# When Pool takes a power, and when it scatters: the graph stage of a decoder

## The chip, the cores and the metric

One core of a Trainium2 chip runs the whole network in one launch. The metric is the device time in microseconds of that launch, as the median of three runs. The engines have queues of their own and run in order: TensorE (PE), VectorE (DVE), ScalarE (ACT), GpSimd (Pool) and SyncE (SP), which issues most of the transfers. They meet only at semaphores.

## The reference, cut to what matters

The network is two decoder layers on x of shape (4, 512, 512). The change touches one stage, the graph attention of the first layer and the routing of the mixture of experts that follows it, for each of 4 batches of 512 rows:

```python
sim = einsum('bhnd,bhmd->bnm', Q, K) / (sqrt(d) * H)
threshold = top_k(sim, int(512 * 0.3))[0][:, :, -1:]      # the 153rd largest of each row
A = sigmoid(sim) * (sim >= threshold)
A = (A + swapaxes(A, -1, -2)) * 0.5
x = x + (1 - gamma) * layernorm(x) + gamma * A            # layernorm(x) stands for adj_raw
scores = softmax(layernorm(x) @ w_cls.T)                  # 64 experts, 32 of them real
_, choice = top_k(scores + bias, 8)                       # 8 experts a row
```

The normalised rows go to the slots of their experts, 8 copies of each.

## The kernel before

The stage is the function graph_and_router. A batch is four tiles of 128 rows. PE makes the similarities, and the 153rd largest of each row is found in two ways at once. For tiles 0 and 1 (COUNTED) it is found by halving: ACT counts in 32 rounds (TESTS) how many similarities lie above a test value (`count`, L1896, two instructions a round, one for each tile), and after each count Pool moves the test (`update`, L2220 to L2236, two to four small instructions a tile). For tiles 2 and 3 DVE takes the eight largest and strikes them out, 20 times (`strike_out`, L2000 and L2006). The search of batch b + 1 is interleaved with the rest of batch b's work on DVE by an order written out by hand in `finish` and `router`.

DVE's order for a batch b is: `blend_statistics(b)`, the mean and variance of x (the last instruction is L2025); `blend_x(b)`, which waits for Pool's power and makes the sum of x and its normalised self (L2034 to L2044); `exact_bounds(b)`, which waits for the last update of batch b (the flags, L2051); `adjacency(b)` (L2069, L2072); two rounds of the next search; `add_adjacency(b)`, which waits for PE's transposed adjacency; the statistics of the new x; two more rounds; `normalize(b)`, which waits for Pool's second power (L2089); five rounds; the router, from the logits (L2125) to the slots (L2184); the remaining rounds. In the last batch there is no next search.

Pool raises the variances to the power -1/2 in `rstds(b, k)` (L2240), k = 0 for x and k = 1 for the x with the adjacency added. It also sends the normalised rows to their slots: `scatter` (L2248) is an indirect DMA of 128 rows, and there are 32 for each batch. The 32 of batch b are spread over the rounds of the next two batches: ten go behind rounds 22 to 31 (LATE) of batch b + 1, the rest in the early rounds (EARLY) of batch b + 2. For the last two batches what is left goes behind the last round. ACT also copies, in its order, the queries, keys and similarities of batch b + 1 behind round 4 of batch b (round 2 of batch 0), the transposed x, the logits and the exponentials of batch b - 1 behind rounds 9, 11 and 13, and results of other weight work that fills PE (`keep_aside`, behind rounds 18 to 29). PE runs in the order of the batches: transposed adjacency, similarities of batch b + 2, logits, counts of choices, weight work. SP reloads x for the next batch behind `blend_x` and stores the sum behind `add_adjacency`.

The stage ends when all scatters have landed. The experts' stage reads the slots.

Of the kernel before, what the change touches and what calls it, by code (L numbers as in the profile page):

```python
# [16 lines left out]
B, S, D = 4, 512, 512  # L17
T = B * S
NT = S // P
# [1523 lines left out]
def graph_and_router(nc, env, tag, x_in, x_out, ctx_in, wq, wk, gamma, w_cls, bias, slot_rows, none_row, slots, weights, w1, w3, w2, hadamard, w13T, w2T, late_jobs, first_gu, first_d, shared_x, shared_rows, w_gate_up, w_down):  # L1543

    with semaphores(nc) as take, ExitStack() as ctx:
# [424 lines left out]
        def _(dve):  # L1970
# [94 lines left out]
            def adjacency(b):  # L2065
                for t in range(NT):
                    dve.wait_ge(tanh_done, NT * b + t + 1)
                    least = bound[:, t:t + 1] if t < COUNTED[b] else top[:, t, LAST:LAST + 1]
                    dve.tensor_scalar(sim[:, b % 2, t, :], sim[:, b % 2, t, :], least, gam[:, 2:3], ALU.is_ge, ALU.mult).then_inc(masked, 1)  # L2069
                for t in range(NT):  # L2070
                    dve.wait_ge(masked, NT * b + t + 1)
                    dve.scalar_tensor_tensor(out=adjacent[:, t, :], in0=adjacent[:, t, :], scalar=1.0, in1=sim[:, b % 2, t, :],  # L2072
                                             op0=ALU.add, op1=ALU.mult).then_inc(adj, 1)
# [18 lines left out]
            def finish(b):  # L2092
                exact_bounds(b)
                adjacency(b)
                strike_out(b + 1, 0, 2)
                if b < B - 1:
                    add_adjacency(b)
                    dve.wait_ge(added, NT * (b + 1))
                    carry()
                    statistics(b, 1, xo)  # L2100
                else:
                    for t in range(NT):
                        add_tile(b, t)
                        dve.wait_ge(added, NT * b + t + 1)
                        carry()
                        tile_statistics(1, xo, t)
                    gather_statistics(b, 1)
                strike_out(b + 1, 2, 4)
                normalize(b)
                strike_out(b + 1, 4, 9)  # L2110
                router(b, lambda: strike_out(b + 1, 9, 10), lambda: strike_out(b + 1, 10, ROUNDS + 1))
# [80 lines left out]
            strike_out(0, 0, ROUNDS + 1)  # L2192
            for b in range(B):
                blend_statistics(b)
                blend_x(b)
                finish(b)
            for u, (j, c) in enumerate(late_units):
                high, low = late_jobs[j][1:]
# [8 lines left out]
        def _(pool):  # L2207
# [30 lines left out]
            def rstds(b, k):  # L2238
                pool.wait_ge(stat[k], (2 * NT + 1) * (b + 1))
                pool.tensor_tensor(rstd[:, k, :, 0], mv[:, k, :, 1], env.minus_half[:, 0:NT], ALU.pow).then_inc(rstd_done[k], 1)  # L2240
# [22 lines left out]
            LATE = 22  # L2263
            EARLY = {0: 2, 4: 5, 5: 1, 7: 1, 9: 3, 10: 1, 11: 2, 13: 2, 15: 1, 17: 1, 18: 1, 20: 1, 21: 1}
            assert sum(EARLY.values()) + TESTS - LATE == NT * TOPK
            for b in range(B):
                sent = TESTS - LATE
                for r in range(TESTS):
                    for j in range(COUNTED[b]):
                        update(b, r, j)  # L2270
                    if b and r == 4:
                        rstds(b - 1, 1)
                    if r == (26 if b else 24):
                        rstds(b, 0)
                    if b >= 2 and r in EARLY:
                        scatter(b - 2, sent, sent + EARLY[r])
                        sent += EARLY[r]
                    if b and r >= LATE:
                        if b == 1 and r == LATE:
                            pool.wait_ge(zeroed, 16 * (ZERO_DMAS + 1))  # L2280
                        scatter(b - 1, r - LATE, r - LATE + 1)
            scatter(B - 2, TESTS - LATE, TESTS - LATE + 12)
            rstds(B - 1, 1)
            scatter(B - 2, TESTS - LATE + 12, NT * TOPK)
            scatter(B - 1, 0, NT * TOPK)
            for i in range(2):
                pool.wait_ge(scattered[i], 16 * NT * TOPK * B // 2)
# [611 lines left out]
```

## Time and profile before

| | us |
|---|---|
| median of 3 runs | 3081.89 |
| lowest and highest | 3077.84, 3084.49 |
| the profiled execution | 3076.68 |
| its span, first to last instruction | 3074.7 |
| graph stage, first search to last scatter (of the span) | about 690 to 1196 |
| busy over the span: PE, DVE, ACT, Pool | 2470.5, 1837.2, 1242.4, 859.5 |
| mean granted TensorE clock | 0.893 |

The profile gives for each instruction its engine, start and length in us from the start of the span, and what ended the idle time of its engine before it. Times without another mark are such starts. Idle time of an engine counts only if something waits for the engine later.

### The profile page before, as it was taken

To read this page: it belongs to the slowest core of one execution; us is meant where nothing else is said; L and a number is where in the kernel's file an instruction comes from. 1 tells how busy PE (TensorE), PEld (TensorE's weight loads), DVE (VectorE), ACT (ScalarE), POOL (GpSimd) and SP (SyncE) were. 2 spreads that over 40 slices of the span, in tenths; PEclk is the share of its full clock that TensorE was granted. 3 is DMA by queue.
4 is the path that set the end of the run, shared out by engine and by line. 5 is a ranking of instruction groups with operands and counts; after the bars stand their busy time and mean duration, and the time that the engine had idled before them with its cause. 6 is when DMAs were issued, how large, how long until landed. Compare 5 with 4: busy or idle time off the path is not lost. (4 is left out here: it accounts for less than half of the span.)

```text
span 3074.7 us, 34907 instructions
## 1 busy us (share of the span) xinstructions
PE 2470.5 (80%) x12662; PEld 1631.8 (53%) x12662; DVE 1837.2 (60%) x2917; ACT 1242.4 (40%) x1873; POOL 859.5 (28%) x1198
## 2 busy tenths in 40 slices
PE   5898989863531334999727999999999969999999
PEld 4454545321211223999624545545555537888887
DVE  3756566528977853777556777565555534444443
ACT  2443435328745533666402334334333323333332
POOL 2222223215667755333263333001111110000000
PEclk8999999975665666999858999999999979999999
DMA  4213131226222153899676565333433324001000
GB/s 121 58 43 83 42 82 46 69 103 265 76 70 83 58 166 113 287 304 304 209 188 160 133 178 146 101 83 95 121 100 79 100 74 159 31 11 42 1 28 14
DMA packets 200952, 340.40 MB, mean 111 GB/s; under 512 B 28809, under 2 KB 60425, under 8 KB 198754
## 3 DMA queue, kind: packets, MB, share of 16 engines
q1 hardware_dynamic: 177250, 299.80, 32.3%
q0 software_dynamic: 20480, 37.87, 4.9%
q8 instruction: 86, 1.41, 0.2%
q10 hardware_dynamic: 3072, 0.79, 0.1%
q14 instruction: 64, 0.52, 0.1%
HBM read 182.30 MB, written 109.05 MB: 95 GB/s over the span
## 5 line engine op out<-in xcount | busy, mean ns | idle before, releaser
L670 ACT ACTIVATE at_probs<-at_ps 128x1024 f32<-128x1024 f32 (+3 forms) x256 | 221.8, 866 | 273.7 <-PE at_ps L538 271.0
L757 DVE TENSOR_REDUCE at_negmax<-at_ps 128x2 f32<-128x1024 f32 (+3 forms) x256 | 259.0, 1015 | 122.0 <-PE at_ps L523 64.3
L1367 DVE TENSOR_REDUCE a_negmax<-a_ps 128x2 f32<-128x1024 f32 x128 | 155.1, 1216 | 137.4 <-PE a_ps L1120 136.8
L1896 ACT ACTIVATE gr_act_signs<-gr_signed,gr_test 128x512 bf16<-128x512 f32 x248 | 177.2, 716 | 133.4 <-POOL gr_test L2236 103.1
L59 PE MATMUL ff_ps<-ff_xnT_hi,ff_s_hi 128*128 128x512 f32 x512 | 201.0, 393 | 5.1 <-DVE ff_xnT_lo L2767 5.1
L61 PE MATMUL ff_ps<-ff_xnT_hi,ff_s_lo 128*128 128x512 f32 x512 | 200.2, 391 | 0.0
L60 PE MATMUL ff_ps<-ff_xnT_lo,ff_s_hi 128*128 128x512 f32 x512 | 200.1, 391 | 0.0
L538 PE MATMUL at_ps<-at_qk 98*128 98x512 f32 (+3 forms) x512 | 172.7, 420 | 20.5 <-DMA at_qk<-at_mrow 11.5
L2797 DVE TENSOR_TENSOR ff_hid<-ff_hid,ff_ps 128x512 f32<-128x512 f32 x64 | 44.0, 687 | 238.8 <-ACT ff_hid L2742 238.8
L1268 ACT ACTIVATE a_probs<-a_ps 128x1024 f32<-128x1024 f32 x128 | 131.0, 1024 | 137.1 <-PE a_ps L1138 136.6
L518 PE MATMUL at_ps<-at_qk 96*128 96x512 f32 (+3 forms) x512 | 163.9, 384 | 17.7 <-DVE at_xnT_lo L818 8.0
L538 PEld LDWEIGHTS at_ps<-at_qk 98*128 98x128 f32 x512 | 83.6, 195 | 164.6 <-issue 94.4
L2742 ACT ACTIVATE ff_hid<-ff_ps 128x512 f32<-128x512 f32 x64 | 38.3, 598 | 303.5 <-PE ff_ps L61 303.5
L2539 POOL TENSOR_TENSOR ex_d_lo<-first_d,ex_d_hi 128x1024 fp32r<-128x1024 f32 x32 | 95.9, 2996 | 216.8 <-ACT ex_d_hi L2465 216.8
L59 PE MATMUL ex_ps<-ex_x_hi,ex_gu_hi 128*128 128x256 f32 x512 | 148.3, 290 | 0.0
L61 PE MATMUL ex_ps<-ex_x_hi,ex_gu_lo 128*128 128x256 f32 x512 | 145.6, 284 | 0.0
L60 PE MATMUL ex_ps<-ex_x_lo,ex_gu_hi 128*128 128x256 f32 x512 | 145.6, 284 | 0.0
L2248 POOL DMA_INDIRECT slot_rows<-shared_x,slots x128 | 133.0, 1039 | 39.5 <-issue 39.5
L852 POOL TENSOR_SCALAR_AFFINE_SELECT at_probs<-at_probs 128x256 f32<-128x256 f32 x128 | 52.5, 411 | 292.5 <-ACT at_probs L670 292.5
L782 DVE RECIPROCAL at_weighed<-at_weighed 128x128 f32<-128x128 f32 x128 | 119.7, 939 | 15.5 <-ACT at_weighed L705 15.5
L873 POOL TENSOR_TENSOR at_oT<-at_weighed 128x512 f32<-128x512 f32 x32 | 40.7, 1273 | 296.5 <-DVE at_weighed L782 296.5
L726 ACT CAST at_part<-at_ps 128x512 fp32r<-128x512 f32 x64 | 37.5, 587 | 208.9 <-PE at_ps L61 198.4
(410 smaller groups left out, 6552.9 us busy)
## 6 DMA issues: line engine op xcount, KB each, us to landing
at_qk<-at_part SPq DMA_DIRECT2D x384, 128.0 KB, 2.5
first_gu<-in_L_ffn_w_gate_up_dram SPq DMA_DIRECT2D x32, 1024.0 KB, 5.5
a_qk<-a_part SPq DMA_DIRECT2D x192, 128.0 KB, 2.4
slot_rows<-gr_zeros SPq DMA_DIRECT2D x16, 1024.0 KB
first_d<-in_L_ffn_w_down_dram SPq DMA_DIRECT2D x32, 512.0 KB, 6.4
ex_rows<-slot_rows SPq DMA_DIRECT2D x32, 512.0 KB, 4.5
out_rows<-ex_y SPq DMA_DIRECT2D x32, 512.0 KB, 3.0
gr_aside_raw<-in_L_ffn_W_dram SPq DMA_DIRECT2D x48, 256.0 KB, 3.0
```

The costliest lines, as they stand in the source:

```text
L59: pe.matmul(out, lh, rh, start=start, stop=False, skip_group_check=True)
L60: pe.matmul(out, lh, rl, start=False, stop=False, skip_group_check=True)
L61: return pe.matmul(out, ll, rh, start=False, stop=stop, skip_group_check=True)
L518: mm = pe.matmul(bank(key, i, 0, n), qk[0:KROWS, g % STACKS, 0, j, t * P:(t + 1) * P], qk[0:KROWS, g % STACKS, 1, j, 0:n], start=True, sto ...
L538: mm = pe.matmul(bank(key, i, lo), qk[0:KROWS + 2, g % STACKS, 1, j, t * P:(t + 1) * P], qk[0:KROWS + 2, g % STACKS, 0, j, lo:S], start=Tr ...
L670: act.activation(probs[:, t % 2, 2 * w:2 * w + 2, lo:S], banks(("kq", g, s), lo), ACT.Exp, scale=SCALE).then_inc(free(("kq", g, s)), 1)
L757: dve.reduce_max(negmax[:, g % 2, :].rearrange("p (j t) -> p j t", t=NT)[:, 2 * w:2 * w + 2, t], banks(("qk", g, s), 0, width(g, t)), AX.X ...
L782: dve.reciprocal(weighed[:, 1, t * P:(t + 1) * P], weighed[:, 1, t * P:(t + 1) * P]).then_inc(rec_done, 1)
L1268: act.activation(probs[:, t % 2, 2 * w:2 * w + 2, :], banks(("kq", g, s)), ACT.Exp, scale=SCALE).then_inc(free(("kq", g, s)), 1)
L1367: dve.reduce_max(negmax[:, g % 2, :].rearrange("p (j t) -> p j t", t=NT)[:, 2 * w:2 * w + 2, t], banks(("qk", g, s)), AX.X, negate=True).t ...
L1896: act.activation(act_signs[:, j, :], src, ACT.Sign, scale=-1.0, bias=against, accum_out=total[:, i, j:j + 1]).then_inc(counted_to[j], 1)
L2248: pool.indirect_dma_start(slot_rows, bass.IndirectOffsetOnAxis(slots[:, n:n + 1], 0), xn[:, b % 2, at // TOPK, :], None, bounds_check=SLOT ...
```

## The change

Three things. The order of DVE: `blend_x(b)` comes behind `adjacency(b)` and no longer behind the statistics. Pool's powers: `rstds(b, 0)` leaves round 24 (batch 0) or 26 (others) and follows the last round of its batch; `rstds(b - 1, 1)` goes from round 4 to round 8 in batch 1 and to round 5 in batches 2 and 3. Pool's scatters: in the last batch rounds 22 to 31 send none, and the ten of batch 2 that stood there follow behind the last round and the power. There the order is now `scatter(B - 2, 0, 12)`, the second power, `scatter(B - 2, 12, 32)`, where it was `scatter(B - 2, 10, 22)`, the second power, `scatter(B - 2, 22, 32)`.

```diff
--- before.py
+++ after.py
@@ -2092,6 +2092,7 @@
             def finish(b):
                 exact_bounds(b)
                 adjacency(b)
+                blend_x(b)
                 strike_out(b + 1, 0, 2)
                 if b < B - 1:
                     add_adjacency(b)
@@ -2192,7 +2193,6 @@
             strike_out(0, 0, ROUNDS + 1)
             for b in range(B):
                 blend_statistics(b)
-                blend_x(b)
                 finish(b)
             for u, (j, c) in enumerate(late_units):
                 high, low = late_jobs[j][1:]
@@ -2268,20 +2268,19 @@
                 for r in range(TESTS):
                     for j in range(COUNTED[b]):
                         update(b, r, j)
-                    if b and r == 4:
+                    if b and r == (8 if b == 1 else 5):
                         rstds(b - 1, 1)
-                    if r == (26 if b else 24):
-                        rstds(b, 0)
                     if b >= 2 and r in EARLY:
                         scatter(b - 2, sent, sent + EARLY[r])
                         sent += EARLY[r]
-                    if b and r >= LATE:
+                    if 0 < b < B - 1 and r >= LATE:
                         if b == 1 and r == LATE:
                             pool.wait_ge(zeroed, 16 * (ZERO_DMAS + 1))
                         scatter(b - 1, r - LATE, r - LATE + 1)
-            scatter(B - 2, TESTS - LATE, TESTS - LATE + 12)
+                rstds(b, 0)
+            scatter(B - 2, 0, 12)
             rstds(B - 1, 1)
-            scatter(B - 2, TESTS - LATE + 12, NT * TOPK)
+            scatter(B - 2, 12, NT * TOPK)
             scatter(B - 1, 0, NT * TOPK)
             for i in range(2):
                 pool.wait_ge(scattered[i], 16 * NT * TOPK * B // 2)
```

## Rows read from the trace of the kernel before

**Rows 1.** Waits, 690 to 1197 us: total us, times, longest.

```profile
POOL gr_rstd L2240 <- DVE gr_mv L2025: 48.0, 6, 15.6
...
DVE gr_dve_flags L2051 <- POOL gr_test L2236: 45.2, 4, 11.9
```

**Rows 2.** Timeline, Pool, batches 1 to 3: start, length; idle before.

```profile
859.32 1.05 POOL L2240 TENSOR_TENSOR gr_rstd<-gr_mv,minus_half 128x4 f32<-128x4 f32 x1 [15.65 <-DVE gr_mv L2025]
...
976.91 1.05 POOL L2240 TENSOR_TENSOR gr_rstd<-gr_mv,minus_half 128x4 f32<-128x4 f32 x1 [8.76 <-DVE gr_mv L2025]
...
1094.18 1.05 POOL L2240 TENSOR_TENSOR gr_rstd<-gr_mv,minus_half 128x4 f32<-128x4 f32 x1 [9.03 <-DVE gr_mv L2025]
```

**Rows 3.** Timeline, DVE: the first flags of batches 1, 2 and 3.

```profile
874.62 0.74 DVE L2051 TENSOR_SCALAR_CACHE_REDUCE gr_dve_flags<-gr_signed,gr_test 128x512 bf16<-128x512 f32 x1 [11.75 <-POOL gr_test L2236]
...
992.34 0.74 DVE L2051 TENSOR_SCALAR_CACHE_REDUCE gr_dve_flags<-gr_signed,gr_test 128x512 bf16<-128x512 f32 x1 [11.88 <-POOL gr_test L2236]
...
1109.64 0.75 DVE L2051 TENSOR_SCALAR_CACHE_REDUCE gr_dve_flags<-gr_signed,gr_test 128x512 bf16<-128x512 f32 x1 [11.91 <-POOL gr_test L2236]
```

**Rows 4.** Timeline, DVE: the adding of a tile in batch 1, and a blend.

```profile
889.29 0.69 DVE L2078 TENSOR_TENSOR shared_rows<-shared_rows,gr_ps 128x512 f32<-128x512 f32 x1 [1.07 <-PE gr_ps L1774]
...
978.54 1.92 DVE L2044 TENSOR_SCALAR shared_rows<-first_d,gr_blend 128x512 f32<-128x512 f32 x4
```

**Rows 5.** Timelines, batch 1: normalising, round 8, logits, slots, round 22.

```profile
790.66 0.55 DVE L2089 TENSOR_SCALAR shared_x<-shared_rows,gr_mv,gr_rstd 128x512 f32<-128x512 f32 x1
...
797.81 0.38 POOL L2232 TENSOR_SCALAR gr_steps<-gr_powers,gr_base 128x23 f32<-128x23 f32 x1
...
806.77 0.42 DVE L2125 TENSOR_REDUCE gr_r<-gr_ps 128x4 f32<-128x256 f32 x1 [0.31 <-PE gr_ps L1794]
...
829.63 0.18 DVE L2184 CAST slots<-gr_k 128x32 int32<-128x32 f32 x1
...
831.26 0.34 POOL L2236 TENSOR_SCALAR gr_test<-gr_half,gr_steps,gr_test 128x1 f32<-128x1 f32 x1
```

**Rows 6.** Timeline, Pool: rounds 25, 26 (batch 1), 26 (batch 2).

```profile
840.42 0.34 POOL L2236 TENSOR_SCALAR gr_test<-gr_half,gr_steps,gr_test 128x1 f32<-128x1 f32 x1
...
843.33 0.34 POOL L2236 TENSOR_SCALAR gr_test<-gr_half,gr_steps,gr_test 128x1 f32<-128x1 f32 x1
...
967.82 0.34 POOL L2236 TENSOR_SCALAR gr_test<-gr_half,gr_steps,gr_test 128x1 f32<-128x1 f32 x1
```

**Rows 7.** Timelines, ACT and Pool: rounds 4 to 6, batches 2, 3.

```profile
899.71 0.71 ACT L1896 ACTIVATE gr_act_signs<-gr_signed,gr_test 128x512 bf16<-128x512 f32 x1
...
905.48 0.32 POOL L2226 TENSOR_SCALAR gr_half<-gr_total,gr_offset 128x1 f32<-128x1 f32 x1
...
1007.84 0.27 POOL L2227 TENSOR_SCALAR gr_test<-gr_half,gr_test 128x1 f32<-128x1 f32 x1
...
1022.41 0.33 POOL L2226 TENSOR_SCALAR gr_half<-gr_total,gr_offset 128x1 f32<-128x1 f32 x1
```

**Rows 8.** Timeline, Pool: updates beside the adjacency and a blend.

```profile
878.59 2.78 POOL L2221 TENSOR_SCALAR gr_sign<-gr_half 128x1 f32<-128x1 f32 x1
...
753.82 0.70 POOL L2236 TENSOR_SCALAR gr_test<-gr_half,gr_steps,gr_test 128x1 f32<-128x1 f32 x1
```

**Rows 9.** Timeline, ACT: rounds 20, 21 and 23 of batch 3.

```profile
1065.34 0.72 ACT L1896 ACTIVATE gr_act_signs<-gr_signed,gr_test 128x512 bf16<-128x512 f32 x1 [0.94 <-POOL gr_test L2236]
...
1067.23 0.72 ACT L1896 ACTIVATE gr_act_signs<-gr_signed,gr_test 128x512 bf16<-128x512 f32 x1
...
1072.84 0.72 ACT L1896 ACTIVATE gr_act_signs<-gr_signed,gr_test 128x512 bf16<-128x512 f32 x1 [0.93 <-POOL gr_test L2236]
```

**Rows 10.** Timeline, Pool: the tail behind the last batch's flags.

```profile
1128.67 1.08 POOL L2240 TENSOR_TENSOR gr_rstd<-gr_mv,minus_half 128x4 f32<-128x4 f32 x1
...
1154.55 0.56 POOL L2246 TENSOR_TENSOR gr_pool_carrier<-minus_half 128x1 f32<-128x1 f32 x1 [11.68 <-DVE slots L2184]
...
1195.19 0.97 POOL L2248 DMA_INDIRECT slot_rows<-shared_x,slots  x1 [0.30 <-issue]
```

## Prediction

> **What bounds the kernel now.** I read the page first: the span is 3074.7 us and its slices show the graph stage (about 690 to 1196 us) with Pool and DVE busy and PE mostly idle. All edits lie there. Then the waits of that stretch [rows 1]: Pool stands 48.0 us in six waits for DVE's variances, DVE 45.2 us in four waits for Pool's last updates of the tests, and ACT, which counts, for Pool in each round. The reader is to see a triangle: Pool stands still for DVE, ACT stands still for Pool, and then DVE stands still for both. The timelines show where. In batches 1, 2 and 3 Pool meets `rstds(b, 0)` at round 26, before DVE has finished its search (`strike_out`), and idles 15.65, 8.76 and 9.03 us [rows 2]. DVE then finishes, blends x, and idles 11.75, 11.88 and 11.91 us until Pool and ACT have made rounds 27 to 31 [rows 3]. I call the start of a batch's flags (L2051) F(b): F1 = 874.62, F2 = 992.34, F3 = 1109.64. Whatever comes after F3 hangs on DVE, then on Pool's scatters, which end at 1196.2 [rows 10]; DVE and SP have nothing left there from 1172 us on, so Pool's scatters alone end the stage. A gain counts if it moves F3 or shortens the tail behind it.
>
> **What the edits do, one by one.** No instruction is added or removed; eight powers, 16 blends and 128 scatters stand elsewhere.
>
> *Batch 0.* The power leaves round 24 for the place behind round 31. There it cost one power, 1.05 us as in [rows 2], and a few tenths of slower updates beside the blend: about 1.2 us. Everything behind it comes 1.2 us earlier. Moving `blend_x` behind `adjacency` puts 2.5 us (three small operations and 1.92 us, [rows 4]) on DVE, ahead of `strike_out(b+1, 0, 2)` (5.6 us). What hides it: DVE waits behind those for PE's transposed adjacency, 1.07 us in batch 1 before tile 3 and as much before tile 4 [rows 4]. The last tile sets the end, and DVE with 2.5 us more work in front still reaches it in time (rounded cost 0 to 0.2 us a batch; without PE's cover 2.5 us each). SP's reload of x waits for the blend, which is 80 us ahead of its reader: nothing.
>
> *Batch 1: the late power of the sum.* `rstds(0, 1)` moves from round 4 to round 8. In before it ran while ACT was copying the next similarities, at no cost; DVE normalised at 790.66 as soon as its search rounds let it [rows 5]. Round 8 ends on Pool at 798.19, 797.0 with the 1.2 us; the power ends at 798.05. So DVE starts `normalize(0)` at 798.1, 7.4 us later than in before, a new stall of some 8.5 us. Behind this wait stand DVE's search, the router and, over PE's transposes and logits, ACT's copies at rounds 9, 11 and 13. From 790.66 to the end of x's variances at 859.23 (0.1 us before the power at 859.32, [rows 2]) DVE has 0.31 us of waits [rows 5]; so they end at 798.1 + 68.6 - 0.3 = 866.4. Pool and ACT: ACT's copies wait for the late normalising (3 us at round 9), and its exponential at round 13 for DVE (until 815.0, against 809.2 in before), so round 22 ends at 831.6 + 5.9 = 837.5, just behind DVE's slots (829.8 + 7.1 = 836.9) [rows 5]. A round with a scatter takes 843.33 - 840.42 = 2.91 us [rows 6]; nine of them give 863.7. DVE is later: **F1 = 866.4, 8.2 us earlier** (with the power left at round 4 it would be about 16).
>
> *Batch 2.* Pool makes 5 scatters of round 4 at once, where it stood until 894.94 for variances, but round 5 must wait for ACT, which is busy with the copies: its counts of round 5 end at F1 + 25.1 (899.71 + 0.71) [rows 7]. Update 1.35, power 1.05: `normalize(1)` starts at F1 + 27.6 against + 25.7 [rows 7], a stall of 2 us. Round 6 starts at + 28.9 with its scatter, in before at 905.48 = + 30.9: counting runs 1.9 us ahead. The logits come by ACT at rounds 9 and 11, so DVE's wait for them (5.51 us in before) swallows its stall and DVE runs 1.9 us ahead too: variances at + 102.2 - 1.9 = + 100.3. Round 26 ended at 968.16 = + 93.5 [rows 6], so now + 91.6; round 31 is five rounds of 2.91 on, its first column 0.7 us less: + 105.5. Here counting decides: **F2 = 866.4 + 105.5 = 971.9, 20.4 us earlier.** F2 - F1 falls from 117.7 to 105.5; the rest of Pool's 8.76 us wait is gone and 3.4 us come from the overlap.
>
> *Batch 3.* Pool's last scatter and the power delay its first updates to F2 + 3.3 against + 2.1. They now meet DVE's adjacency, which holds Pool [rows 8], so rounds 1 to 4 are 1.3 us later: round 4 ends at + 17.1 instead of 1008.14 = + 15.8 [rows 7]. Five scatters of 1.28 us: + 23.5. ACT copies no similarities in this batch, so round 5 follows at once, then the power, which ends at + 26.2; `normalize(2)` is 1.3 us late (1017.29 = + 24.95). Round 6 starts at + 27.5 against 1022.41 = + 30.1: 2.5 us ahead, and again the logits (5.52 us of DVE waiting) pass it on. DVE's variances, in before at 1094.1 = + 101.8, are at **F2 + 99.3**. Rounds 23 to 31 lose their scatters: with a copy from the aside work ACT needs 1067.23 - 1065.34 = 1.89 us a round [rows 9], where 2.91 was paid. Round 23 starts at 1072.84 [rows 9] (+ 80.5, now + 78.0); seven rounds of 1.89, one of 1.67, 1.6 us for two waits for PE's mixing and 1.5 us for the last count and update give + 96.0, below + 99.3: hidden, 3 us to spare. **F3 = 971.9 + 99.3 = 1071.2, 38.4 us earlier.** Had the scatters stayed, + 78 + 8 x 2.91 + 1.5 = + 102.8 would have been the bound, so their move is worth 3.5 us here.
>
> *The tail.* Pool makes the power at F3 + 1, then 12 scatters: 12 x 1.28 + 1.5 for one that meets the adjacency = up to + 19.3, then the second power. In before it began at 1128.67 = + 19.0 [rows 10], with 12 scatters in front as well, since 10 had gone out in the rounds. DVE's variances are there at + 16.7. The blend fits the 2.7 us wait for PE, if PE's first tile comes no later. Then 20 scatters (in before 10): 25.6 us, to + 45.9, where batch 3's slots are ready at 1154.55 = + 44.9 and Pool idled 11.68 us [rows 10]. So the extra 10 scatters (12.8 us) go into that idle time and 1 us sticks out. Bounds of the tail: - 1 us to + 4 us (PE cold in the transposes, DVE's first wait longer, two scatters held); I take + 0.5.
>
> The sum is 38.4 - 0.5 = 37.9 us from the profiled time of 3076.68 (span 3074.7 and 2 us around it). The median of the three is 3081.89, 5.2 us more; I take the change from it: **3044.0 us**.
>
> Pool is held by DVE in one kind of place: while DVE makes `adjacent` from two inputs (2.49 us), a Pool update takes 2.78 instead of 0.2 us; beside a blend (one input) one takes 0.70 instead of 0.34 [rows 8]. I charge the blends 0.3 us per update. The Trainium skill (SBUF — State Buffer, "SBUF: two separate sides") says that the pair of ports is an exclusive lock, taken by DVE operations in a two-port mode or with two inputs, and that the loser fully blocks. By that, each moved blend would stop the first rounds of the next batch's counting for 1.9 us instead of 0.6; only F2 hangs on counting, so by the page the sum would be 1.3 us smaller. The row of the two-input operation agrees with the full stop, that of the blend shows less.
>
> **The rivals.** (a) *Round 8 costs all of batch 1's gain.* If ACT's stalls at rounds 9 and 13 are 11 us longer than I charge, round 31 ends at 874.6 and F1 does not move. For it: three engines wait in turn. Against it: what ACT waits for is work of 2 to 6 us whose rows I have added already. 8.2 us go: 3052, and 3060 if batch 2 meets the same. (b) *Only batch 3 gains.* If Pool's waits merely move behind round 31 and hold the next batch's start by as much, batches 1 and 2 keep their length and 18 us remain: 3064. Against it: behind round 31 Pool waits 2.3 us in batch 1 and not in batch 2. (c) *No change*: DVE's search and router are already the bound and its 11.8 us idle are refilled by later waits for the powers; 3080. Against it: those waits sum to 12 us, of 47 that go. (d) *Slower*: a run of scatters costs more when it begins right at the search's end, as transfers crowd. 64 stand behind F3 against 54. In before they take 1.28 us each, one beside the adjacency 2.77. It decides from 1.9 us each on (0.6 x 64 = 38 us); at 2.2 us each the stage is 59 us longer behind F3 and the time 3103. Against it: 54 in a row at 1.28.
> (e) *More*: the late power is covered (DVE and ACT overlap better); 46 us, 3036.
>
> **How the numbers follow.** Chances: the sum within 8 us 0.60, (a) 0.14, (b) 0.08, (c) 0.06, (d) 0.06, (e) 0.06. The predicted time is the sum's. The range takes the sum's case and (a) and (e): 3034 to 3060. A measurement here tells 0.2%, 6 us, from no change. Faster: 0.60 + 0.14 + 0.08 + 0.06 = 0.88; same 0.06; slower 0.06.
>
> **What would show it.** Pool's idle time before L2240 under 10 us in all; DVE's before L2051 near 8.5 (batch 0), 0, 5 and 0 us; a new DVE wait of 8 us before L2089 in batch 1; F3 near 1071; Pool's last scatter near 1158; Pool's idle before the last batch's slots gone. It is wrong if F1 is not before 870, if ACT's rounds behind 22 in batch 3 stay above 2.2 us, or if Pool reaches the last batch's slots more than 3 us late.

## The result, and the profile after

The changed kernel takes 3040.2 us (median of 4 runs, 3039.4 to 3045.0) beside 3081.3 for the kernel before: the ratio is 0.987, with a 95% interval of 0.9855 to 0.9886. The prediction was 3044.0, within 3034 to 3060. The profiled execution takes 3039.4 us, its span is 3037.4 against 3074.7.

I read the waits of the graph stage first, to compare them with [rows 1]. This is the changed kernel, 686 to 1155 us of the span; total us, times, longest:

```profile
POOL gr_rstd L2240 <- DVE gr_mv L2025: 5.0, 3, 3.2
...
DVE gr_dve_flags L2051 <- POOL gr_test L2236: 18.8, 2, 14.0
...
DVE shared_x L2089 <- POOL gr_rstd L2240: 11.2, 3, 8.0
...
ACT gr_act_signs L1896 <- POOL gr_test L2236: 53.4, 42, 4.9
```

Pool's waits for the variances went from 48.0 to 5.0 us, DVE's for the last update from 45.2 to 18.8. The third line is the new wait that the prediction named. The fourth shows that the circle is broken on ACT's side too: ACT waited 103.1 us for this line of Pool's updates before, 53.4 now. The work is the same, only the standing still is gone; the stretches between the batches' flags show it. First the changed kernel, batch 1, batch 2, batch 3 and the tail:

```profile
core 0: us, PE busy (x) PEld busy (x) DVE busy (x) ACT busy (x) POOL busy (x), PEclk, DMA share, GB/s
758.00:860.00 102.00, 38.34 (x140) 22.38 (x140) 90.23 (x259) 68.33 (x168) 62.63 (x152) 0.65 0.27 88
860.00:967.00 107.00, 40.94 (x140) 22.86 (x140) 91.52 (x268) 62.35 (x154) 81.35 (x169) 0.64 0.25 81
967.00:1066.00 99.00, 34.90 (x130) 20.74 (x131) 90.99 (x262) 60.82 (x155) 73.82 (x163) 0.62 0.27 83
1066.00:1162.00 96.00, 40.12 (x190) 26.87 (x188) 46.13 (x115) 17.52 (x31) 68.60 (x68) 0.68 0.39 129
```

The same stretches of the kernel before:

```profile
core 0: us, PE busy (x) PEld busy (x) DVE busy (x) ACT busy (x) POOL busy (x), PEclk, DMA share, GB/s
765.00:874.00 109.00, 39.10 (x140) 21.35 (x140) 90.47 (x262) 64.58 (x160) 60.25 (x146) 0.64 0.26 82
874.00:992.00 118.00, 37.91 (x140) 20.96 (x140) 91.03 (x262) 64.59 (x161) 84.14 (x173) 0.63 0.24 78
992.00:1109.00 117.00, 36.04 (x128) 21.00 (x128) 91.29 (x262) 60.06 (x152) 83.90 (x171) 0.59 0.21 65
1109.00:1203.00 94.00, 37.62 (x190) 25.96 (x190) 43.31 (x107) 19.33 (x35) 58.72 (x61) 0.70 0.41 131
```

DVE is busy for the same 90 to 92 us in each batch, but the batches are 102, 107 and 99 us long, not 109, 118 and 117. In the third, DVE is now busy for 92% of the time: there it is the bound.

The starts of the flags answer to [rows 3], and of the powers to [rows 2]. Timelines of the changed kernel, DVE and Pool, in order of time (lines below the diff stand one lower than before, so the logits' reduction is L2126):

```profile
758.23 0.74 DVE L2051 TENSOR_SCALAR_CACHE_REDUCE gr_dve_flags<-gr_signed,gr_test 128x512 bf16<-128x512 f32 x1 [13.98 <-POOL gr_test L2236]
...
792.27 1.92 DVE L2089 TENSOR_SCALAR shared_x<-shared_rows,gr_mv,gr_rstd 128x512 f32<-128x512 f32 x4 [7.98 <-POOL gr_rstd L2240]
...
860.37 0.74 DVE L2051 TENSOR_SCALAR_CACHE_REDUCE gr_dve_flags<-gr_signed,gr_test 128x512 bf16<-128x512 f32 x1
...
860.55 1.05 POOL L2240 TENSOR_TENSOR gr_rstd<-gr_mv,minus_half 128x4 f32<-128x4 f32 x1 [1.11 <-DVE gr_mv L2025]
...
888.62 1.92 DVE L2089 TENSOR_SCALAR shared_x<-shared_rows,gr_mv,gr_rstd 128x512 f32<-128x512 f32 x4 [2.10 <-POOL gr_rstd L2240]
...
967.00 0.74 DVE L2051 TENSOR_SCALAR_CACHE_REDUCE gr_dve_flags<-gr_signed,gr_test 128x512 bf16<-128x512 f32 x1 [4.84 <-POOL gr_test L2236]
...
1010.66 0.42 DVE L2126 TENSOR_REDUCE gr_r<-gr_ps 128x4 f32<-128x256 f32 x1 [2.02 <-PE gr_ps L1794]
...
1066.00 0.74 DVE L2051 TENSOR_SCALAR_CACHE_REDUCE gr_dve_flags<-gr_signed,gr_test 128x512 bf16<-128x512 f32 x1
...
1066.18 1.04 POOL L2240 TENSOR_TENSOR gr_rstd<-gr_mv,minus_half 128x4 f32<-128x4 f32 x1 [3.20 <-DVE gr_mv L2025]
...
1084.62 1.04 POOL L2240 TENSOR_TENSOR gr_rstd<-gr_mv,minus_half 128x4 f32<-128x4 f32 x1 [0.67 <-DVE gr_mv L2025]
...
1113.60 0.22 POOL L2246 TENSOR_TENSOR gr_pool_carrier<-minus_half 128x1 f32<-128x1 f32 x1
...
1153.63 0.97 POOL L2248 DMA_INDIRECT slot_rows<-shared_x,slots  x1 [0.30 <-issue]
...
1161.97 0.88 SPq L2353 DMA_DIRECT2D ex_rows<-slot_rows  x2
```

F1 to F3 are 860.37, 967.00 and 1066.00. The flags of batches 1 and 3 begin with no idle time, those of batch 2 after 4.84 us: DVE bound, counting bound, DVE bound, as the sum had it. The power behind round 31 waits for the variances for 1.11 us, nothing and 3.20 us, where [rows 2] had 15.65, 8.76 and 9.03. In batch 3 DVE waits 2.02 us for the logits, where it waited 5.52 before: that slack took up the late normalising. In the tail Pool goes from batch 2's last scatter to batch 3's first without idle time (in [rows 10] it idled 11.68 us), and the last scatter ends 88.6 us behind F3.

| us | before | after | difference | foreseen |
|---|---|---|---|---|
| stage begins (first count) | 693.4 | 686.8 | -6.6 | 0 |
| first count to F0 | 71.2 | 71.5 | +0.3 | -1.2 |
| F0 to F1 | 110.1 | 102.1 | -7.9 | -7.0 |
| F1 to F2 | 117.7 | 106.6 | -11.1 | -12.2 |
| F2 to F3 | 117.3 | 99.0 | -18.3 | -18.0 |
| F3 to the last scatter's end | 86.5 | 88.6 | +2.1 | +0.5 |
| to the experts' first load | 7.4 | 7.4 | 0 | 0 |
| from that load to the end | 1871.1 | 1875.4 | +4.3 | 0 |

Each row is a difference of starts in the two timelines; the stage itself, first count to last scatter, is 34.9 us shorter. The first and the last row hold only instructions that both kernels have in the same order. In the thirteen executions read here that hold all the work the stage begins between 686.8 and 696.4 us whatever the kernel, so the 6.6 us are no part of the change. From the load to the end it is 1869.8 to 1877.5 us in the same thirteen, so the 4.3 us are none either. Of the 3040.2 us measured against 3044.0 foreseen, some of the nearness is therefore luck: the stage gained 3 us less than foreseen, and the execution that was read began it 6.6 us early.

### The profile page after: what moved, and what is told of

It is laid out like the page before. It is cut to its first block and busy times, and to the rows that moved or that the text cites. A ratio compares the mean times of both kernels' runs of the same rounds, so it can differ in the third digit from the quotient of the medians.

```text
span 3037.4 us, 34907 instructions
## 1 busy us (share of the span) xinstructions
PE 2468.5 (81%) x12662; PEld 1636.9 (54%) x12662; DVE 1837.5 (60%) x2917; ACT 1242.0 (41%) x1873; POOL 855.3 (28%) x1198
## 5 line engine op out<-in xcount | busy, mean ns | idle before, releaser
L1896 ACT ACTIVATE gr_act_signs<-gr_signed,gr_test 128x512 bf16<-128x512 f32 x248 | 177.2, 716 | 81.5 <-POOL gr_test L2236 53.4
L518 PE MATMUL at_ps<-at_qk 96*128 96x512 f32 (+3 forms) x512 | 162.4, 381 | 19.5 <-DVE at_xnT_lo L818 8.9
```

Source lines behind the costliest of these rows:

```text
L518: mm = pe.matmul(bank(key, i, 0, n), qk[0:KROWS, g % STACKS, 0, j, t * P:(t + 1) * P], qk[0:KROWS, g % STACKS, 1, j, 0:n], start=True, sto ...
L1896: act.activation(act_signs[:, j, :], src, ACT.Sign, scale=-1.0, bias=against, accum_out=total[:, i, j:j + 1]).then_inc(counted_to[j], 1)
```

## The experiments

The three distances between the flags repeat within 0.4 us from one execution of the changed kernel to another, and within 1.5 us in the kernel before (117.3 and 118.7 us from F2 to F3), so a single profile tells parts apart that the whole time doesn't. All diffs stand against the changed kernel, if nothing else is said.

**1. Both kernels again.** Nothing edited, both on one other chip.

> The kernel before, unchanged, for a second trace. The profile of the changed kernel begins the graph stage 6.6 us earlier (first count of ACT at 686.7 instead of 693.4 us) and loses 4.3 us again behind the experts, on lines that the change does not touch. Theory: both are variation from execution to execution; then this trace begins the stage somewhere between 686 and 694 us, and F1 to F3 stand 117.7 and 117.3 us apart as before, within 0.5. Rival: the change shifts them through the layout of the program; then this trace repeats 693.4 within 1 us.

> The changed kernel, unchanged, for a second trace and a narrower interval. Theory (variation): the stage begins anywhere between 686 and 694 us, and inside it the distances repeat within 0.5 us (F1 to F2 106.6, F2 to F3 99.0, F3 to the last scatter 88.6); time 3040 to 3043, 38 to 41 us less than before. Rival (layout): begins at 686.7 again, within 1 us.

The kernel before took 3083.0 us there (median of 7; the execution with a profile 3085.9), the changed one 3056.4 (4 runs): 0.9909, interval 0.9892 to 0.9925. I had expected 3040 to 3043 for the changed one and was wrong. The start of the stage varies, as expected (689.1 and 694.8 us), and the kernel before has 109.3, 118.0 and 118.7 us between the flags, the last 1.4 us more than in its first execution, where I had expected 0.5 at most. The distances of the changed kernel are 102.5, 106.9 and 99.2 us, within 0.4 us of the first execution, and the stage is 39.4 us shorter than in the kernel before there (508.9 to 469.5). But the experts' first load comes 19.0 us behind the last scatter, and 12.7 in the kernel before, where both had 7.4. The timelines show what ends the stage in that case. First execution of the changed kernel, DVE's last work of the stage and the load:

```profile
1124.90 2.47 DVE L2201 COPY at_wo<-gr_ps 128x512 f32<-128x512 f32 x4
...
1161.97 0.88 SPq L2353 DMA_DIRECT2D ex_rows<-slot_rows  x2
```

Its repeat on the other chip:

```profile
1089.37 1.05 PE L1774 MATMUL gr_ps<-ident,gr_adjacent 128*128 128x128 f32 x8
...
1092.03 0.69 DVE L2078 TENSOR_TENSOR shared_rows<-shared_rows,gr_ps 128x512 f32<-128x512 f32 x1 [1.90 <-remote]
...
1144.65 1.12 PE L1823 MATMUL gr_ps<-ident,gr_aside_raw 128*128 128x128 f32 x4 [7.55 <-issue]
...
1163.25 0.98 POOL L2248 DMA_INDIRECT slot_rows<-shared_x,slots  x1 [0.30 <-issue]
...
1164.34 0.59 ACT L1916 COPY gr_aside_w<-gr_ps 128x512 f32<-128x512 f32 x1 [10.61 <-remote]
...
1177.54 2.47 DVE L2201 COPY at_wo<-gr_ps 128x512 f32<-128x512 f32 x4
...
1183.27 0.88 SPq L2353 DMA_DIRECT2D ex_rows<-slot_rows  x2
```

In the first, the next layer's weights (`at_wo` is the last of them) are ready 34.6 us before the load, and Pool's scatters end the stage. In the repeat they are ready 3.3 us before it: they end the stage. ACT stood 10.61 us in front of L1916, a copy of the other weight work that is ahead of them in its order: PE's transposes for it end at 1145.77 by the trace, and ACT starts at 1164.34, 18.6 us later. The same chain in the repeat of the kernel before, where its links are easy to read: DVE subtracts, PE transposes, ACT casts.

```profile
1175.68 0.69 DVE L2204 TENSOR_TENSOR at_wk_lo<-gr_ps,at_wk_hi 128x512 fp32r<-128x512 f32 x1 [4.27 <-ACT at_wk_hi L1967]
...
1176.43 1.12 PE L1858 MATMUL gr_ps<-ident,gr_signed 128*128 128x128 f32 x4 [3.78 <-issue]
...
1180.01 0.59 ACT L1967 CAST at_wk_hi<-gr_ps 128x512 fp32r<-128x512 f32 x1 [4.36 <-remote]
```

DVE ends at 1176.37 and PE starts 0.06 us later; PE's matmuls end at 1177.55 by the trace and ACT starts 2.46 us after that, where the other hand-overs of this kind take 0.04. So the hand-over behind PE's matmuls is late; the others are not. The delays begin when Pool has issued scatters without a break for 10 to 15 us, grow to 7.3 us in the kernel before and to 18.6 in the changed one, and the last of them ends 4 to 5 us behind the last scatter. DVE meets them too: above, PE's last tile of the transposed adjacency ends at 1090.42 and DVE starts on it at 1092.03. By such waits the last batch's slots are ready 46.0 to 48.7 us behind F3 in the executions with late hand-overs and 44.4 to 44.8 in the others. The eight profiles of experiments 1 to 5, on two chips, all have them, and none of the other six has. Experiments 6 and 7 look for the cause.

**2. The second power at round 4 again, and behind round 4's scatters.** What is round 8 (and 5) worth? One kernel puts the power back where it was:

```diff
-                    if b and r == (8 if b == 1 else 5):
+                    if b and r == 4:
                         rstds(b - 1, 1)
```

and one puts it behind the scatters of round 4:

```diff
-                    if b and r == (8 if b == 1 else 5):
-                        rstds(b - 1, 1)
                     if b >= 2 and r in EARLY:
                         scatter(b - 2, sent, sent + EARLY[r])
                         sent += EARLY[r]
+                    if b and r == 4:
+                        rstds(b - 1, 1)
```

> The changed kernel with the power of the sum back at round 4 in all batches. Theory: in batch 1 DVE's stall of 8.0 us before normalising goes and F1 comes 7.5 us earlier against the start of the stage; in batch 2 Pool stands again for the variances, so F1 to F2 grows from 106.6 to 107.4, and F2 to F3 from 99.0 to 101.8. Sum: 3.9 us less than the changed kernel, about 3036. Rival: the late round 8 costs nothing, because ACT and Pool bound batch 1 in any case; then F1 stays and the kernel is 3.6 us slower than the changed one, about 3044.

> The changed kernel with the power of the sum behind round 4, in batches 2 and 3 behind the five scatters of that round. Theory: F1 comes 7.5 us earlier as in the run with round 4; in batch 2 the power lies in the time in which Pool waits for ACT's copies, so DVE's stall of 2.1 us goes, round 6 comes 1 us earlier and F1 to F2 is 105.6; F2 to F3 stays 99.0. Sum: 8.5 us less than the changed kernel, about 3032. Rival (round 8 costs nothing): within 2 us of the changed kernel.

The first took 3051.5 us (3045.8 to 3055.7; 0.9891, 0.9875 to 0.9908), the second 3044.5 (3041.9 to 3047.7; 0.9874, 0.9858 to 0.9891), on the chip where the changed kernel takes 3056.4 (0.9892 to 0.9925). So the second is faster than the changed kernel; for the first the intervals overlap. The 3036 and 3032 us of the expectations were not met, since the hand-overs are late here. From F0 to F1 they need 93.8 and 94.9 us instead of 102.1. Timeline of the first, with the power, the normalising and the flags of batch 1, then the power in batch 2:

```profile
783.57 1.04 POOL L2240 TENSOR_TENSOR gr_rstd<-gr_mv,minus_half 128x4 f32<-128x4 f32 x1 [5.78 <-DVE gr_mv L2025]
...
788.94 0.56 DVE L2089 TENSOR_SCALAR shared_x<-shared_rows,gr_mv,gr_rstd 128x512 f32<-128x512 f32 x1
...
857.08 0.74 DVE L2051 TENSOR_SCALAR_CACHE_REDUCE gr_dve_flags<-gr_signed,gr_test 128x512 bf16<-128x512 f32 x1
...
877.53 1.05 POOL L2240 TENSOR_TENSOR gr_rstd<-gr_mv,minus_half 128x4 f32<-128x4 f32 x1 [6.41 <-DVE gr_mv L2025]
```

The wait of 7.98 us before the normalising is gone, and F1 comes 8.3 us earlier (7.3 in the second kernel). Pool does stand still again (5.78 us here), as in the kernel before, but beside ACT's copies of the similarities, where it holds nobody up. In batches 2 and 3 the same place costs: Pool waits 6.41 us at round 4 with its scatters behind, and F1 to F2 and F2 to F3 take 107.8 and 102.6 us against 106.6 and 99.0. Behind the scatters, the power is ready when it is asked for, and the distances are 104.5 and 99.3. So round 8 costs 7 to 8 us, as forecast, and the best place in the later batches is behind round 4's scatters.

**3. The powers alone, the scatters alone.** The first keeps the last batch's scatters in rounds 22 to 31:

```diff
-                    if 0 < b < B - 1 and r >= LATE:
+                    if b and r >= LATE:
...
-            scatter(B - 2, 0, 12)
+            scatter(B - 2, TESTS - LATE, TESTS - LATE + 12)
             rstds(B - 1, 1)
-            scatter(B - 2, 12, NT * TOPK)
+            scatter(B - 2, TESTS - LATE + 12, NT * TOPK)
```

The second is the kernel before with only those ten scatters moved (its diff is the one above with the signs changed).

> The changed kernel, but the last batch's rounds 22 to 31 send their ten scatters as before. Theory: with 2.91 us a round counting bounds the last batch: F2 to F3 grows from 99.0 to 103 us, and the tail from F3 to the last scatter falls from 88.6 to 86.5. Sum: 1.5 to 2 us more than the changed kernel, about 3042. Rival: the scatters were the larger part of the gain; then F2 to F3 is near 110 and the kernel 10 us slower than the changed one.

> The kernel before, with only the ten scatters of the last batch's rounds 22 to 31 moved behind the search; both kinds of powers and the blend stay where they were. Theory: Pool still stands at round 26 until DVE's search ends, so only the five rounds behind it gain, 1 us each: F2 to F3 falls from 117.3 to 112, and the tail grows from 86.5 to 88.5 us. Sum: 3 to 4 us less than before, about 3078. Rival (scatters are the larger part): 15 us or more less than before.

With the powers alone F2 to F3 is 104.0 us and the flags of batch 3 stand 4.91 us for counting:

```profile
1071.47 0.75 DVE L2051 TENSOR_SCALAR_CACHE_REDUCE gr_dve_flags<-gr_signed,gr_test 128x512 bf16<-128x512 f32 x1 [4.91 <-POOL gr_test L2236]
```

So the scatters' move is worth 5.0 us there. With the scatters alone F2 to F3 is 111.4 us, 5.9 less than in the kernel before and 7.3 less than in its repeat. The tails, from F3 to the last scatter, are 90.4 us with the powers alone (expected 86.5) and 91.7 with the scatters alone (expected 88.5): late hand-overs make them longer. The whole times show little of it: 3052.1 us for the powers alone (3046.8 to 3057.3, 0.9902, 0.9885 to 0.9918), no different from the changed kernel's 0.9909 on a chip with the same late hand-overs; and 3087.6 for the scatters alone, 1.0006 (0.9995 to 1.0017, 10 runs), no change. The profiles say where a part goes: the ten scatters lengthen the unbroken run, the late weights end later, and the load comes 11.2 us behind the last scatter with the powers alone but 19.0 us with both; 16.0 us with the scatters alone against 12.7 in the kernel before.

**4. The blend ahead of the flags again.**

```diff
             def finish(b):
                 exact_bounds(b)
                 adjacency(b)
-                blend_x(b)
...
                 blend_statistics(b)
+                blend_x(b)
                 finish(b)
```

> The changed kernel with the blend of x back ahead of the flags, so DVE waits there for the power that now stands behind round 31. Theory: each batch pays the power and the blend on DVE's path: F0 + 4.2, F1 to F2 and the batches behind it + 3.75, + 5.9 and + 3.75 us; 17 us more than the changed kernel, about 3057. Rival: the blend behind the adjacency is not covered by PE's transposes; then it costs its 2.5 us in either place and this kernel is only 5 us slower than the changed one (the powers' 1 us a batch), about 3045.

It took 3065.8 us (3061.2 to 3071.4; 0.9942, 0.9926 to 0.9959). First count to F0 is 75.5 us against 71.5, F0 to F1 105.3 against 102.1, F1 to F2 111.8 against 106.6. Timelines, batch 2, Pool and DVE:

```profile
981.63 1.07 POOL L2240 TENSOR_TENSOR gr_rstd<-gr_mv,minus_half 128x4 f32<-128x4 f32 x1
...
983.27 1.92 DVE L2044 TENSOR_SCALAR shared_rows<-first_d,gr_blend 128x512 f32<-128x512 f32 x4
...
985.10 0.74 DVE L2051 TENSOR_SCALAR_CACHE_REDUCE gr_dve_flags<-gr_signed,gr_test 128x512 bf16<-128x512 f32 x1
```

With the power behind round 31, a blend ahead of the flags waits for the end of counting and then puts 3.5 us between it and the flags. From F2 to F3 nothing is lost (98.8 us), where I had expected 3.75 more. The two moves belong together: the power's without the blend's gives back some 12 us by F2. The time is 9.4 us above the changed kernel's on the other chip with late hand-overs, neither the 17 us of the theory nor the 5 of the rival.

**5. The best order found.** The kernel of experiment 2 with the power behind round 4's scatters, and two scatters ahead of the first power in the last batch, where Pool waits 3.20 us for variances:

```diff
+                if b == B - 1:
+                    scatter(B - 2, 0, 2)
                 rstds(b, 0)
-            scatter(B - 2, 0, 12)
+            scatter(B - 2, 2, 14)
             rstds(B - 1, 1)
-            scatter(B - 2, 12, NT * TOPK)
+            scatter(B - 2, 14, NT * TOPK)
```

> The kernel with the power of the sum behind round 4, and in the last batch two of the ten moved scatters ahead of the first power, in the 3.2 us in which Pool waits there for DVE's variances; 12 follow the power as before and 18 instead of 20 the second one. Theory: Pool reaches the last batch's slots 2.5 us earlier (it is 3.2 us late in the changed kernel), the tail falls from 88.6 to 86.1 us: 11 us less than the changed kernel, about 3029. Rival: the tail's 2 us come from scatters held by DVE's two-input operations, not from their number; then the tail stays near 88 us.

3040.4 us (3036.9 to 3048.2) beside 3085.5 before: 0.9867, 0.985 to 0.9883. From first count to last scatter it takes 459.0 us, 8.9 less than the changed kernel. It ran on a chip with late hand-overs, where the changed kernel has 0.9909 (0.9892 to 0.9925, on another such chip); the intervals don't meet, though the two were not timed side by side. The tail did not fall to 86.1 us, as I had expected: it is 89.7, 1.4 less than in experiment 2's kernel with the same place of the power (91.1, the other chip with late hand-overs). PE's late hand-overs have the slots ready only 48.0 us behind F3, and now Pool is there first and waits 0.87 us for them.

**6. Does Pool's unbroken run make the hand-overs late?** Pauses in the last batch's run, in `scatter`:

```diff
+                    if b == B - 1 and at % 8 == 0:
+                        pool.wait_ge(scattered[0], 16 * NT * TOPK * B // 2)
+                        pool.wait_ge(scattered[1], 16 * (NT * TOPK * (B // 2 - 1) + at))
```

and a kernel without that run:

```diff
-            scatter(B - 1, 0, NT * TOPK)
-            for i in range(2):
-                pool.wait_ge(scattered[i], 16 * NT * TOPK * B // 2)
+            pool.wait_ge(scattered[0], 16 * NT * TOPK * B // 2)
+            pool.wait_ge(scattered[1], 16 * NT * TOPK * (B // 2 - 1))
```

> The changed kernel with four pauses of Pool in the last batch's run of scatters: before the 1st, 9th, 17th and 25th it waits until every scatter issued so far has landed (the computation is the same). In the repeat of the changed kernel Scalar waited 4 to 11 us at a time for signals behind the last search (in its first execution at most 1.8 us) while Pool issued scatters without a break, and the experts' first load came 19.0 us behind the last scatter, not 7.4; the work that ends the stage there is the transposes of the next layer's weights, done 3.3 us before that load, not 35 us. Theory A (the unbroken run of scatters makes the other signals late, and a break lets them catch up): Scalar's waits for the late weights fall under 3 us each, those weights are done over 15 us before the last scatter, each pause costs the landing, some 2 us, so 8 us in all, and the load follows the last scatter by 7 to 12 us: the time is between 8 us less and 2 us more than the repeat's 3056. Theory B (it is the chip's or the session's, and has nothing to do with Pool): the waits stay at 4 to 11 us, the weights still end 3.3 us before the load, and the pauses add up to 8 us. Theory C (what makes them late is how many scatters have been issued in all, not the break): as B, but the waits begin later by the pauses.

> The changed kernel without the last batch's 32 scatters, so that the rows of that batch never reach the experts' table (left out: those rows; all else is computed). Theory A (the run of scatters makes the signals late): behind the last of batch 2's scatters Scalar's late weights go through without a wait over 2 us, as in the first execution (11 us from the first to the last of them, where the repeat of the changed kernel without this edit had its last at 1180.0), and the experts' first load comes some 3 us behind them, 45 to 55 us behind the last batch's flags instead of 109. Theory B (not Pool): the waits of 4 to 11 us stay, and the weights end 60 us or more behind the flags.

With pauses: 3051.6 us (3044.4 to 3058.7; 0.9914, 0.9898 to 0.9929; before 3076.0 there); the load comes 7.4 us behind the last scatter and the weights are ready 43 us before it. One of the four pauses, in the timeline:

```profile
1130.86 0.97 POOL L2251 DMA_INDIRECT slot_rows<-shared_x,slots  x1 [0.30 <-issue]
...
1133.78 0.97 POOL L2251 DMA_INDIRECT slot_rows<-shared_x,slots  x1 [1.95 <-DMA slot_rows<-shared_x,slots]
```

Without the run: 3010.5 us in one execution. ACT casts the late weights without a wait over 1.2 us, they are ready at 1131.0 and the load comes 3.6 us later, 64.6 us behind F3 (1069.96). I had said 45 to 55 for that distance, and was wrong: with nothing late the weights end 61 us behind F3, as in the changed kernel's first execution (1127.37 - 1066.00). Both results agree with theory A, but they don't tell it from B, since the chip may show nothing late with any kernel.

**7. The paused and the changed kernel on one chip.**

> The changed kernel, unchanged, on the same chip as the paused one below. Its stage repeats within 1 us up to the last flags (102, 107 and 99 us from batch to batch). Behind them either it runs as in its first execution (the late weights done 30 us or more before the experts' first load, that load 7.4 us behind the last scatter), or as in its repeat (weights done 3.3 us before the load, load 19 us behind the last scatter, 16 us slower in all). If the first, the ratio to the kernel before is near 0.987; if the second, near 0.991.

> The kernel with four pauses in the last batch's run of scatters once more, now beside the changed kernel. In its first run nothing behind the flags was late (weights done 43 us before the load, load 7.4 us behind the last scatter), but neither was anything late in the kernel that only left scatters out, so the chip may simply not have shown it. If the changed kernel beside it shows the late signals: theory A (the unbroken run makes them late) says that here they are gone and that this kernel is 2 to 10 us faster than the changed one; theory B (not Pool) says that they stay and that it is slower than the changed one by the pauses, 8 us. If the changed kernel does not show them, both theories say 8 us slower than the changed one (its last scatter is issued 8.5 us later), and the question stays open.

The changed kernel: 3042.4 us (3038.4 to 3045.5), 0.9876 (0.9856 to 0.9896), distances 102.1, 106.6 and 99.1 us, its load 7.4 us behind the last scatter. The paused one: 3049.5 (3048.8 to 3054.4), 0.9898 (0.9881 to 0.9915), last scatter 8.4 us later. No hand-over was late in either. The pauses cost about what they were priced at (8 us): 8.4 us by the profiles, 7 by the medians, whose intervals just overlap. Whether they would help where the hand-overs are late stays open.

## Why the prediction was right, and where it was off

**What bounds the kernel**: right. Three engines waited in a circle; breaking it at Pool's wait gave three shorter batches with the same work in them. Two of the three signs of being wrong stayed away (F1 is before 870, and ACT's rounds behind 22 in batch 3 take 1.89 us, but for one that waits for PE); the third came: Pool reaches the last batch's slots 3.2 us late, and the limit was 3. It belongs to the tail, below.

**Batch 0**: foreseen 1.2 us earlier, seen +0.3. The 1.2 us are there: rounds 25 to 31 take 12.6 us in all eleven profiles with the power behind round 31 and 13.8 in the three with it behind round 24. But rounds 0 to 24 take 58.1 to 60.3 us, whatever the kernel, 58.1 in the kernel before and 59.6 in the changed one, and that hides it. DVE's idle time before the flags was foreseen at 8.5 us and is 13.98: I took the power off the 9.66 us of before (45.2 in [rows 1] less the three of [rows 3]) and forgot that the blend, and DVE's wait of 1.67 us for its power, leave this very stretch. The idle time costs nothing.

**Batch 1**: the late power is the term that was priced best. Foreseen: DVE stalls until 798.1 and F1 is 8.2 us earlier, about 16 with the power at round 4. Seen: a stall of 7.98 us, F0 to F1 7.9 us shorter, and 8.3 more with the power at round 4 (experiment 2). Rival (a) fell: ACT's own waits hold nothing up.

**Batch 2**: foreseen 105.5 us, counting bound, seen 106.6 and counting bound. The normalising waits 2.10 us (foreseen 2). The 1.1 us over it arise in round 5, and 0.7 of them are a slip of mine: I had ACT's counts of that round end at F1 + 25.1 "(899.71 + 0.71)", but 899.71 + 0.71 less 874.62 is 25.8; + 25.1 is the start of the last count. The other 0.4 us are ACT's copies ahead of it, which end at F1 + 24.8 and not + 24.5. The changed kernel, ACT's last count of round 5 and Pool's first update of round 6:

```profile
885.83 0.71 ACT L1896 ACTIVATE gr_act_signs<-gr_signed,gr_test 128x512 bf16<-128x512 f32 x1
...
890.25 0.47 POOL L2226 TENSOR_SCALAR gr_half<-gr_total,gr_offset 128x1 f32<-128x1 f32 x1
```

The count ends at F1 + 26.2 and round 6 starts at + 29.9, where I had + 28.9: counting runs 1.0 us ahead of the kernel before and not 1.9, and it stays so (round 26 ends at + 92.8, foreseen + 91.6). The blends are not the cause. This row pair has one of them and a Pool update beside it, changed kernel:

```profile
974.14 2.01 DVE L2044 TENSOR_SCALAR shared_rows<-first_d,gr_blend 128x512 f32<-128x512 f32 x4
...
974.24 0.21 POOL L2222 TENSOR_SCALAR gr_offset<-gr_half 128x1 f32<-128x1 f32 x1
```

The update takes 0.21 us inside the blend's 2.01 us. Some others beside a blend take 0.53 to 0.79 us in these runs where 0.3 is usual, and a scatter at most 1.22 for 0.97: slower, but none is held for the whole blend. The Trainium skill (SBUF — State Buffer, "SBUF: two separate sides") has the loser of the shared pair of ports fully blocked for the whole instruction, if the blend takes the pair. A blend is four instructions of 0.54 us, so by that rule an update is held up to 0.5 us at a time, and not 1.9, as I had worked out from it; the update of 0.21 us is not held at all. Beside the adjacency, with two inputs, the rule and the trace agree: an update of Pool takes 2.87 us there, as in [rows 8], and a scatter 2.82.

**Batch 3**: foreseen 99.3, DVE bound, counting 3 us below; seen 99.0, DVE bound, and Pool's power waits 3.20 us for the variances, which is that margin. The scatters' move, priced at 3.5 us, is worth 5.0 (104.0 with them kept; I had 102.8). The rounds take the 2.91 us that I had; the term that was too small is the 1.5 us for the last count and update. With the powers alone, ACT's last round and the scatter of round 30:

```profile
1068.56 0.72 ACT L1896 ACTIVATE gr_act_signs<-gr_signed,gr_test 128x512 bf16<-128x512 f32 x1 [1.39 <-POOL gr_test L2236]
...
1069.56 1.08 POOL L2248 DMA_INDIRECT slot_rows<-shared_x,slots  x1 [0.34 <-issue]
```

The last update has to wait for that scatter, and from the last round's start to the flags (1071.47) it is 2.9 us.

**The tail**: foreseen +0.5, seen +2.1, inside the bounds of -1 to +4. Pool reaches the last slots 3.2 us after they are ready (1110.44), where I had 1 us. The term that was too small is that of the 20 scatters ahead of it, priced at 1.28 us each, 25.6 us: they take 27.9. Of the 2.3 us more, 1.4 are one scatter that now lies beside DVE's router, where Pool idled before, and the rest is in the first scatters and small gaps. That scatter, and what DVE does there:

```profile
1100.81 2.29 DVE L2144 TENSOR_TENSOR gr_hot<-gr_iota,gr_choice 128x2048 f32<-128x2048 f32 x1
...
1101.61 2.34 POOL L2248 DMA_INDIRECT slot_rows<-shared_x,slots  x1 [0.30 <-issue]
```

A scatter costs 0.97 us and its gap, this one 2.34: it ends 0.85 us after DVE's operation of two inputs does. The same section of the Trainium skill says that a VectorE instruction with two inputs in SBUF contends with a GpSimd instruction that reads SBUF, as a scatter does for its slots; by that rule it can be held here, and the row agrees. The section also reports that `tensor_tensor` was not seen to stall a DMA of GpSimd; this row, where it holds one, differs, and the measurement decides. I had used the rule for the blends, where little came of it, and for one scatter beside the adjacency, but not for those that now lie beside the router.

**The sum**: 37.9 us foreseen, 34.9 measured inside the stage. Rival (b) fell by batches 1 and 2, (c) by all three. (d) had one thing right: a longer unbroken run of scatters can cost time. Not in the way it said, since most of them still take 1.28 us, and not in the first execution; where the hand-overs from PE are late, the gap between last scatter and load grows from 12.7 to 19.0 us with the change, which gives back 6.4 of the 39.4 us won in the stage. What makes them late is open: they go with Pool's run in time, and the gap is 16.0 to 19.5 us in the five profiles with 38 or 39 scatters in the last unbroken run (none more than 2 us behind the one before) and 11.2 to 12.7 in the three with 32, but some chips don't show them at all, and the pauses, which would have told, were tried on such chips only.

## What to carry to other kernels

When engines wait for each other in turn, move the request of the one that stands still to where its answer is already there, and move everything that consumes the answer with it: the power without the blend gave back 12 us. A moved request should go no later than its reader: at round 8 it cost 7 to 8 us that round 4 did not, so look for the place that is both after the producer and before the reader, per batch. And look at what else hangs behind a stage's end: work with 30 us to spare on one chip ended the stage on another.

## What the runs showed of the hardware

The same program, with the same distances within 0.4 us up to the last flags, ran with two different ends. On two chips ACT started up to 18.6 us after the end of PE's transposes, once Pool had issued scatters without a break for 10 to 15 us, and DVE up to 3.4 us after that of PE's transposed adjacency; elsewhere it was 0.04 us throughout a run of 39 scatters. The matmuls' ends are modelled in the trace, so it can't say if PE was late itself or only its signal. The hand-overs from ACT to DVE and from DVE to PE, 0.02 and 0.06 us, stayed prompt in the same stretch. I had not expected a delay behind one engine alone, nor that the changed kernel's time would differ by 14 us between chips (3042.4 and 3056.4) while the kernel before differs by 2 on the same two (3081.4 and 3083.0); over all chips the kernel before has 3076.0 to 3085.5.
